# One slot of eight moved from ScalarE to VectorE in a graph attention loop

## What is computed

```
w_m = (efeat @ W_msg  + b_msg ).reshape(E, 16, 16)
w_a = (efeat @ W_attn + b_attn).reshape(E, 16, 16)
h   = feat[src][:, :, None]
e1, e2 = w_m * h, w_a * h                      # the "scaling": one factor for each edge and row
ex  = exp(e2 - segment_max(e2, dst)[dst])
ft  = segment_sum(e1 * ex / segment_sum(ex, dst)[dst], dst)
x   = layernorm(x + ft.sum(axis=1))
```

## Time and profile before

| | us |
|---|---|
| median of three runs | 2493.0 |
| lowest and highest of them | 2475.16 and 2502.27 |
| span of the profiled execution | 2500.2 |
| the edge part in that span | about 750 to 2462 |
| VectorE busy, whole span | 1976.0 (79%) |
| TensorE busy, whole span | 1885.7 (75%) |
| ScalarE busy, whole span | 1478.0 (59%) |
| GpSimd busy, whole span | 1365.0 (55%) |

### The profile page before, as it was taken

How to read it: one execution, slowest core, us unless ns; L and a number is a source line. 1 busy time by engine, 2 the same in 40 slices (tenths; PEclk the granted TensorE clock), 3 DMA queues, 4 the chain that set the end, 5 groups by cost and what they waited for, 6 DMA issues and landing times.

```text
span 2500.2 us, 37693 instructions
## 1 busy us (share of the span) xinstructions
PE 1885.7 (75%) x5814; PEld 721.8 (29%) x5815; DVE 1976.0 (79%) x3222; ACT 1478.0 (59%) x5049; POOL 1365.0 (55%) x1593
## 2 busy tenths in 40 slices
PE   3666656589717778887888787788888888888865
PEld 1111111133403333333333333333333333333322
DVE  5999999930227788888888788788888888888865
ACT  5347721211136667776776676677776677777752
POOL 1414405655365556665666565566666666666650
PEclk9889998889658888988888888888998888889877
DMA  1010000010001000000000000000000000000000
GB/s 26 23 29 0 1 1 7 8 24 12 17 8 10 9 9 10 10 9 9 10 10 9 9 9 9 9 9 10 10 9 10 10 9 9 10 9 10 9 6 7
DMA packets 85441, 25.80 MB, mean 10 GB/s; under 512 B 61870, under 2 KB 82464, under 8 KB 85280
## 3 DMA queue, kind: packets, MB, share of 16 engines
q0 software_dynamic: 36672, 18.09, 6.0%
q1 hardware_dynamic: 45359, 6.52, 1.7%
q10 hardware_dynamic: 3376, 0.83, 0.2%
HBM read 22.74 MB, written 2.51 MB: 10 GB/s over the span
## 4 chain that ended last, share of the span: by engine, by line
PE 33%; issue 22%; ACT 16%; DVE 14%; DVEq 7%; another core or an unknown queue 4%; ACTq 2%; DMA 1%; SPq 0%; PEldq 0%; PEld 0%
PE pair L868 14%; ACT eo L1104 12%; DVE hot L1283 6%; PE pw L855 5%; PE pair L864 3%; PE pt L837 3%; PE pw L741 2%; PE pw L748 1%; PE pw L745 1%; DVEq L1666 1%; PE bank L699 1%; DVE rden L1642 1%; DVEq L1279 1%; DVE top L1593 1%
## 5 line engine op out<-in xcount | busy, mean ns | idle before, releaser
L641 POOL DMA_INDIRECT nbr<-table,rec x928 | 956.1, 1030 | 563.3 <-ACT eo L1104 292.5
L868 PE MATMUL pair<-eo,ident 128*128 128x512 f32 x1856 | 870.6, 624 | 2.9 <-DVE eo L1624 1.8
L1104 ACT ACTIVATE eo<-pw,nbr 128x32 f32<-128x32 f32 x3712 | 721.5, 357 | 211.7 <-issue 202.1
L868 PEld LDWEIGHTS pair<-eo,ident 128*128 128x128 f32 x1856 | 379.2, 206 | 532.3 <-issue 532.2
L1578 DVE TENSOR_TENSOR eo<-pw,nbr 128x1024 f32 (+1 forms) x348 | 410.3, 1219 | 124.4 <-remote 58.9
L855 PE MATMUL pw<-wk,termsT 100*128 100x512 bf16 x928 | 338.8, 458 | 157.4 <-issue 130.0
L1283 DVE TENSOR_SCALAR hot<-iota_key,near_key 128x500 bf16<-128x500 f16 x974 | 277.8, 348 | 13.3 <-issue 7.5
L1624 DVE TENSOR_TENSOR eo<-eo (+1 forms) x232 | 272.7, 1216 | 1.9 <-ACT eo L1093 1.7
L1615 DVE TENSOR_TENSOR eo<-eo,bank 128x2048 f32 (+1 forms) x116 | 265.4, 2288 | 8.6
L837 PE MATMUL pt<-identb,terms 128*100 128x128 bf16 x928 | 106.9, 246 | 209.8 <-issue 74.3
L1080 ACT CAST termsT<-pt 100x512 bf16<-100x512 f32 x232 | 134.3, 579 | 202.3 <-remote 101.8
(11 more groups left out here) (251 smaller groups left out, 1750.0 us busy)
## 6 DMA issues: line engine op xcount, KB each, us to landing
nbr<-table,rec POOLq DMA_INDIRECT x928
rec<-unit_recs SPq DMA_DIRECT2D x116, 8.0 KB
attr<-in_edge_attr_dram,rec POOLq DMA_INDIRECT x116
unit_recs<-place SPq DMA_DIRECT2D x27, 64.0 KB
shared<-key_row SPq DMA_DIRECT2D x1, 1600.0 KB, 6.6
counts<-in_dst_dram SPq DMA_DIRECT2D x1, 448.0 KB
counts<-in_src_dram SPq DMA_DIRECT2D x1, 448.0 KB
place<-in_src_dram,at_i POOLq DMA_INDIRECT x26, 2.7
```

The lines of the kernel that those rows point to most:

```text
L641: pool.indirect_dma_start(nbr[:, b, j * FEAT:(j + 1) * FEAT], None, table, bass.IndirectOffsetOnAxis(ap=rec[:, b, j:j + 1], axis=0)).then_ ...
L868: mm = pe.matmul(total, ident[:], eo[:, ring, j * 2 * CH:(j + 1) * 2 * CH], start=False, stop=(j == SLOT - 1), skip_group_check=True)
L1104: done = act.activation(eo[:, ring, lo:lo + wide], pw[:, j - 4, c * wide:(c + 1) * wide], ACT.Copy, scale=nbr[:, held, j * FEAT + c:j * FE ...
```

## The change

ScalarE now scales slot 7 alone, with 16 instructions in place of 32 (`last_slot` in place of `last_pair`). Slot 6 goes to VectorE, as one instruction over 16 rows of 32 (`scaled_six`), which stands behind `weighted(v)` and `rest_one(v + 4)` and before `finished`. It waits for the last product of its unit (`s_w_act`) and counts up a semaphore of its own, `s_six`. `product` 1 and `gather_rows` wait for `s_six` beside the signal of ScalarE. Before the loops `scaled_six` follows each of the three `scaled`.

```
             def gather_rows(b, u):
 
                 wait(s_scaled, u + 1)
+                wait(s_six, u + 1)
                 wait(s_pair1_act, u + 1)
...
                 elif k == 1:
                     pe.wait_ge(s_pair1_act, seen + SETS)
+                    pe.wait_ge(s_six, seen + SETS)
...
-            def last_pair(ring, held, seen):
+            def last_slot(ring, held, seen):
...
-                for j in range(SLOT - 2, SLOT):
-                    for c in range(FEAT):
+                j = SLOT - 1
+                for c in range(FEAT):
...
+            def scaled_six(ring, held, seen):
+
+                dve.wait_ge(s_w_act, seen + 1)
+                dve.sem_inc(s_settled_dve, 1)
+                j = SLOT - 2
+                h_src = nbr[:, bass.ds(held, 1), j * FEAT:(j + 1) * FEAT].rearrange("p u c -> p (u c)")
+                dve.tensor_tensor(eo[:, bass.ds(ring, 1), j * 2 * CH:(j + 1) * 2 * CH]
+                                  .rearrange("p r (c f) -> p (r c) f", f=2 * FEAT),
+                                  pw[:, j - 4, :].rearrange("p (c f) -> p c f", f=2 * FEAT),
+                                  h_src.unsqueeze(2).broadcast_to([P, FEAT, 2 * FEAT]), ALU.mult).then_inc(s_six, 1)
...
             scaled(0, 0, 0)
+            scaled_six(0, 0, 0)
             dve.drain()
             peaks(0, 0, "first")
-            scaled(1, 1, 1)
-            scaled(2, 2, 2)
+            for u in range(1, 3):
+                scaled(u, u, u)
+                scaled_six(u, u, u)
...
                 if ahead > 3:
                     rest_one(even, here, v + LEAD)
+                if ahead > 2:
+                    scaled_six(third, third, v + 2)
                 if tile is not None:
                     finished(tile, odd)
```

More of the change, by code:

```diff
@@ L320, in gnn_kernel @@
         s_scaled = sem("s_scaled")
+        s_six = sem("s_six")
         s_attr = [sem(f"s_attr{b}") for b in range(SETS)]
@@ L1100, in last_pair @@
                 wide = 2 * FEAT
-                for j in range(SLOT - 2, SLOT):
-                    for c in range(FEAT):
-                        lo = j * 2 * CH + c * wide
-                        done = act.activation(eo[:, ring, lo:lo + wide], pw[:, j - 4, c * wide:(c + 1) * wide], ACT.Copy,
-                                              scale=nbr[:, held, j * FEAT + c:j * FEAT + c + 1])
+                j = SLOT - 1
+                for c in range(FEAT):
+                    lo = j * 2 * CH + c * wide
+                    done = act.activation(eo[:, ring, lo:lo + wide], pw[:, j - 4, c * wide:(c + 1) * wide], ACT.Copy,
+                                          scale=nbr[:, held, j * FEAT + c:j * FEAT + c + 1])
                 done.then_inc(s_pair1_act, 1)
@@ L1118, in _ @@
             for u in range(2):
-                last_pair(u, u, u)
+                last_slot(u, u, u)
                 for half in range(2):
@@ L1130, in act_unit @@
                 if ahead > 1:
-                    last_pair((b + 2) % RING, (b + 2) % SETS, u + 2)
+                    last_slot((b + 2) % RING, (b + 2) % SETS, u + 2)
                 if ahead > 2:
@@ L1164, in _ @@
             dve.sem_inc(s_g3, 2)
-            for s in (s_scaled, s_attr_free, s_tT, s_pair1_act):
+            for s in (s_scaled, s_six, s_attr_free, s_tT, s_pair1_act):
                 dve.sem_inc(s, 4)
```

## The result

The changed kernel takes 2603.0 us, the median of four runs (2587.74 to 2609.95), against 2492.9 for the kernel before (2475.16 to 2502.27). The ratio is 1.044, 95% interval 1.038 to 1.050. The forecast was 2454, with a range up to 2530: sign and range were both wrong.

What follows compares the result with a forecast made beforehand. VectorE's work plus a wait for ScalarE's long burst bounds most units. Terms +68 - 80 - 15 - 8 + 3 - 7 = -39 us, from 2493 to 2454; range 2425 to 2480, 8 in 10: 2422 to 2530.

Steps and rivals of the forecast that it cites:

- the new wait of GpSimd: At `gather_rows`: both signals open 3 to 3.5 us behind `weighted`, not 8.8; the earlier start brings nothing by itself.
- Added to VectorE: One new instruction in each of 113 units, 0.60 us each: +68 us, between +59 and +77.
- What VectorE waits for there: At `scaled_six`: the unit's last product ends some 3.5 us before VectorE comes to it, so no wait, price 0.
- ScalarE's burst: 16 fewer instructions save 2.9 us, 6.1 in a slow unit; VectorE's wait for `middle` loses 80 of 86.3 us.
- The late start behind it and TensorE's product: VectorE's idle time at the scaling: 15 of 25.8 us by "issue" and 8 of 19.2 us for TensorE go.
- What came late next: The product for the second `scaled`, in units where TensorE is at 1.2 GHz: +3 us.
- The new wait of TensorE: Product 1 also waits for `s_six`; `scaled_six` ends early enough, with 5.6 us of cover in the slow unit: price 0.
- Before the loops: VectorE's 15.02 us wait for a product behind ScalarE's second burst falls by half: -7 us, between 0 and 15.
- the wait of L1566: `rest_two` on VectorE waiting for ScalarE's `middle`, 86.3 us in 60 waits: 80 us go, bounds 40 and 86.
- Rival two: Long gather runs, in a tile's second or third unit: 2522 us with twice as many, 2620 with 24; chance 0.16.
- Rival one: In the edge part, something else keeps the pace, so slow units stay at about 13.9 us: 2514 us; chance 0.22.
- Rival three: VectorE pays and gains nothing, its wait moving to L1578: 2561 us, or 2510 with half the waits gone; chance 0.12.

Runs made afterwards that it cites:

- short_after: The changed kernel, with GpSimd waiting at the head of `gather_rows` for the previous unit's last gather, behind this unit's attribute gather: 2471.5 us, ratio 1.002.
- few_before: The kernel before the change, with four of the eight gathers of each unit left out and slots 4 to 7 constant: 2301.3 us, ratio 0.931.
- few_after: The changed kernel, with four of the eight gathers of each unit left out and slots 4 to 7 constant: 2344.9 us, ratio 0.949.
- no_six: The changed kernel without VectorE's new instruction, slot 6 a constant and its signal given at once: 2545.2 us, ratio 1.025.
- pause1_after: The changed kernel, with GpSimd waiting behind each unit's eight gathers until they have landed: 2453.7 us, ratio 0.990.
- pause1_before: The kernel before the change, with GpSimd waiting behind each unit's eight gathers until they have landed: 2446.3 us, ratio 0.989.
- pause2_after: The changed kernel, with GpSimd waiting behind both the fourth and the eighth gather of each unit: 2698.6 us, ratio 1.089.

## Why the prediction was wrong, step by step

**The step that failed** is *the new wait of GpSimd*: "The gathers are for four units ahead, so an earlier start brings nothing by itself". It has no term in the sum. But the late gate had been what broke the runs: ScalarE's burst of 32, slow tail and all, ended 8.0 us into the median unit (8.8 in that of the earlier trace rows), and GpSimd rested until then. With the gate open at 3.2 us it need not stop. Long runs went from 11 to 22 and held units from 12 to 24, which is 76 us more of idle time.

- *Added to VectorE*: right. 683 ns alone (forecast 680); plain units have 0.56 us more work, tile ends 0.76 where only waits over 0.25 us are taken off, some 66 to 70 us in all (forecast 68). The Trainium skill's "VectorE: DVE Perf Modes", in its TRN2 errata, gave 658 ns; the row is 4% above it.
- *What VectorE waits for there*: right, 5.9 us in three waits over 113 units.
- *ScalarE's burst*: right. It takes 2.96 us or less in all 116 units, and the wait of `rest_two` is gone, all 86 us of it (forecast 80).
- *The late start behind it and TensorE's product*: wrong. "Issue" before the scaling rose from 25.8 to 38.2, the product from 19.2 to 21.8, where -15 and -8 were put down. What came late next was not that product only (+3): `rest_one` waits 25.8 us for `high` and 11.0 by "issue", where before it was 17.1 and 5.0.
- *The new wait of TensorE*: right, no wait for `scaled_six` of any size stands in the trace.
- *Before the loops*: wrong. VectorE's timeline there, to be held against the earlier trace rows:

```profile
732.31 0.69 DVE L1593 TENSOR_TENSOR eo<-pw,nbr 128x512 f32<-128x512 f32 x1 [4.36 <-remote]
759.60 1.23 DVE L1581 TENSOR_TENSOR eo<-pw,nbr 128x1024 f32<-128x1024 f32 x1 [26.60 <-remote]
```

The wait was to fall from 15.02 by half, and is 26.60 us, during 50 transfers in a row where before had 41. The first `weighted` starts 13 us later than before, where -7 was put down; 7 of the 13 stand before the first gather, and so before anything that the change touches. The pattern is that of the held units: with a pause behind every eight gathers no wait of 15 us or more is left there, and the stretch is 26 to 33 us shorter.

The range was also added up wrongly. With the bounds that the prediction gives for VectorE's work (77), the wait of L1566 (40) and the stretch before the loops (0), the sum is +17 and the upper end 2510, not 2480.

**The rivals.** Rival two was the right one, in the form it gave least: with a hold in each of 24 tiles it said 2620, and 2603 was measured, with 24 held units. The price of one was high, 9.75 us against 160 / 24 = 6.7, and the rest came from the terms that failed above, so that the time comes so near is in part luck. Its ground for going low, that "the gate itself enforces the rest", is where the argument broke: the gate opens at a fixed time in the unit, but GpSimd is behind it when a run has begun late, and an early gate does not stop it. The point at which it decides was named rightly: short_after has rests of about 1 us, and they are too short. Rival one was wrong: the plain unit's pace was not the matter, ScalarE's tail did go, and few_before runs at VectorE's own pace. Rival three, and with it the Trainium skill's "Perfetto Trace Analysis" ("Optimizing Scalar/DVE Operations"), foretold slower, and it is: but by its mechanism the price is 43 us where nothing is held (few_after against few_before), 7 with full rests and 30 with short ones, and not 110. The direction agrees, the reason does not.

**And the count.** The prediction read 14 waits as seven places. That was right for its kind, idle time before the scaling: 7 units, for 59 us. Counted that way after has 23. With the waits at other lines 12 units were held before, for 84 us. That is as much as the wait for ScalarE on which the whole forecast turned, and it was read as a remainder.

**What stays open.** Shown is that the long waits of the scaling need the stream of gathers (none with four gathers fewer in few_before, one unit in few_after, none with a full rest), and that they grow in number with its long runs. That a run must be long is not shown: no_six has 15 held units beside runs of nine. What inside the chip is held was not seen: rows show TensorE's work issued in time and its signals some 5 to 6.5 us late, and the ends of matmuls are modelled. Whether the profile's own recording takes part wasn't tried. A rest that is taken only where a run is about to grow long wasn't tried either.

## What to carry to other kernels

An engine that opens another's gate late may be the only thing that breaks up a stream of small transfers. Before making it faster, count in GpSimd's timeline how many transfers would follow each other without a rest, and look at whether waits with an unknown releaser already sit at the ends of such runs. If they do, put a rest into the stream first: one wait for the last gather at the end of each unit made both kernels faster than either was, by about 1% (ratios 0.989 and 0.990 of before, with intervals that end at 0.997 and 0.998). Only then ask where a slot is best computed. The best form run is before with a short rest (2441.0, ratio 0.989) or a full one (2446.3); on top of them the change brings nothing.

## What the runs showed of the hardware

- Runs of nine gathers (12 us) with 2.5 us of rest left no unit with over 3 us of idle time before the scaling (pause1_after, pause1_before). In runs of 17, ScalarE, TensorE and VectorE were held together, from 14 to 18 us into the run until up to 3 us behind its last issue in most, for 6.7 us a unit on average in after.
- A transfer can cost more time than it takes: 251 us for 116 transfers of 1.25 us.
- 0.6 us of VectorE work for each unit, with no dependence on anything, cost 116 us in one setting and 10 to 13 in another.
- ScalarE's short instructions from TensorE's results run at 0.18 us each in a piece of 16, in all 116 units of after. In a piece of 32 a slow tail as in the earlier trace rows came in most units of before, in 95 of 96 of them from the 20th instruction or a later one on, in 8 units of pause1_before, and in none of few_before.
- A gather is issued every 1.25 us (0.95 and 0.30 between). A wait for one that was just issued is a rest of about 2.5 us from the end of its issue behind the eighth (pause1_after, 2.35 at the least), and of about 2.2 behind the fourth (pause2_after).
